# Routing in three parts of two, two and one tiles, the last attention ahead of the third projection, and two tiles' rows summed by GpSimd from a copy made by ScalarE

## The chip, the cores and the metric

One core of one Trainium2 chip runs the whole program in one launch. The metric is device time in microseconds. Of three runs of the kernel before, the median is 133.79 us (133.21 to 134.04). The engines are called as in the profile: PE (TensorE), DVE (VectorE), ACT (ScalarE), POOL (GpSimd) and SP (SyncE, which here only issues DMAs).

## The reference

A vision transformer with one layer and a routed feed-forward part, all in f32:

```python
h = patchify(x) @ W_proj.T + b_proj + pos_emb           # 16 images, 36 patches of 768 -> 256
h = concatenate([cls_tok, h])                           # 37 tokens an image, 592 in all
h = h + attention(layernorm(h))                         # 16 heads of 16, causal, 37 x 37, W_out, b_out
xn = layernorm(h)
logits = (xn @ w_red) @ normalized(wg).T                # 8 experts
idx = argmax(softmax(logits)); score = that softmax's largest value
y = gelu(xn @ w1[idx] + b1[idx]) @ w2[idx] + b2[idx]    # 256 -> 1024 -> 256
h = h + y * score
```

## The kernel before

The 592 tokens are five tiles of 128 rows, tile 0 to 4 (the last has 80 rows). The 16 images are eight **pairs**, 0 to 7 (LAST is 7). The program goes through these stages: the patch embedding; the first norm, keys, queries and values; attention pair by pair; the output projection of each tile; the routing of each tile; and the eight experts. Every engine has its own list of instructions, written out by hand, and takes them in that order. Engines meet at semaphores: `wait_ge(q["name"], n)` holds the engine's list until that semaphore has been raised n times.

**Values.** ACT copies each tile's value rows, with eight more columns `xg` (the input's share of the routing logits), to `hz[:, j, 0:264]` (`save_values`, L407). SP stores them to memory and loads them back in another layout (L335, L341), in two halves of four pairs. POOL multiplies each pair's values with a mask into `vbd` (L1118, eight instructions, the last four from the second half).

**Attention** is a loop over i from 1 to 7 on all engines. In step i PE does: scores of pair i (L609, L617), `turned` of pair i-3 (two transposes of the result, L679), `transposed` of pair i-1 (six transposes of the probabilities, L654), `attend` of pair i-2 (24 matmuls in the profile, L672), and in steps 4 and 6 `project` of tile 0 or 1 (L685). DVE takes the maximum and subtracts it (L907, L911), and divides the result of pair i-2 (`weighted`, L969, L972). ACT copies the turned result of pair i-3 out of PSUM (`save_output`, L457, two instructions), the transposed probabilities of pair i-1 (`save_probs`, L465, two) and takes the exponential of pair i (L433). The results of pairs 0 to 5 all use one PSUM bank, so `attend(u)` first waits until `ot_ready` says that ACT's `save_output` of pair u-1 is done (L664).

**Projection and routing.** For tiles 0 to 2 DVE adds the residual rows to the projection (L929); for tiles 3 and 4 PE adds them with a matmul by the identity (`own_row`, L692) and ACT copies them (`second_rows`, L412, L414). The routing logits are eight more columns of the projection; DVE adds `hG` to them (L920), which it made before with one small instruction per tile from `xg` (L994). Then `choose` finds each row's expert (five instructions), PE counts the rows ahead of each (`count_before`, L697 to L703), `keys` and `places` (L953 to L959) make the row's address and a 0/1 matrix, and `dispatch` (L715) multiplies the normalised rows by that matrix, which gives the inputs of experts 0 and 1 on the chip. This is done in two parts, tiles 0 to 2 and tiles 3 and 4. POOL takes the inverse root of each tile's variance (L1124) and writes the normalised rows (L1129). All rows also go to memory by five indirect DMAs (L1138), and SP loads them back for experts 2 to 7 (L354).

**Experts.** `hidden` (L793) and `down` (L807) on PE, with the weights of four experts held at a time. SP issues the weights of expert 4 after the row loads (L326, L327).

Of the kernel before, what the change touches and what calls it, by code (L numbers as in the profile page):

```python
# [20 lines left out]
P = 128  # L21
# [31 lines left out]
EARLY = 3  # L53
# [70 lines left out]
def vit_tower(nc, embed_in, places_in, b_proj, w_qkv, b_qk, b_v, w_out, w_out_t, b_out, b_out_c, wg, w_red_t, w1, b1, w2, b2,  # L124
              cf_d, cb_d, iota_d, out):
    ctx = ExitStack()
    with ctx:
# [142 lines left out]
        PROJ_BANK = (BZ, BZ, BZ, 1, 2)  # L270
# [6 lines left out]
        def o_bank(u):  # L277
# [9 lines left out]
            hb_ready proj_ps veps2_ready rstd2_ready shift2_ready h2_ready z_pool z_act  # L287
            loaded_woutt loaded_boutc gc_ready wg_ps hg_ready
# [101 lines left out]
        def _(act):  # L390
# [25 lines left out]

            def second_keys(a):
# [68 lines left out]
            for j in range(EARLY):  # L486
                weigh(j)
            for j in range(BY_PE, NT):
                second_rows(j)
# [3 lines left out]
            act.wait_ge(q["hot_ready"], 2)  # L493
            for j in range(EARLY, NT):
                weigh(j)
# [25 lines left out]
        def _(pe):  # L521
# [167 lines left out]
            def own_row(j):  # L689
                pe.wait_ge(q["hb_ready"], j + 1)  # L690
                pe.wait_ge(q["hg_ready"], j + 1)
                nc.tensor.matmul(ps[:, PROJ_BANK[j], 0:DV], ident, h[:, j, :], start=True, stop=False)  # L692

            def count_before(j0, j1):
# [3 lines left out]
                pe.wait_ge(q["hot_ready"], 1 if j0 == 0 else 2)  # L698
# [7 lines left out]
            def dispatch(j):  # L706
# [5 lines left out]
                pe.wait_ge(q["place32_dve"], j + 1)  # L712
                for t in range(ONCHIP):
                    for k in range(KD):
                        m = nc.tensor.matmul(ps[:, BX[t][k], 0:P], hz[:, j, D + k * P:D + (k + 1) * P],  # L715
                                             place32[:, j, t * P:(t + 1) * P], start=(j == 0), stop=(j == NT - 1))
                        if j == NT - 1:
                            m.then_inc(q["soon_ps"], 1)

            for i in range(1, PAIRS):  # L720
# [12 lines left out]
                if i in PROJ_AT:  # L733
# [4 lines left out]
                    else:  # L738
                        pe.wait_ge(q["h2_ready"], j)
# [17 lines left out]
            count_before(0, EARLY)  # L757
            pe.wait_ge(q["ot_ready"], KD * PAIRS)
            project(4)
            pe.wait_ge(q["h2_ready"], BY_PE)  # L760
            for j in range(EARLY - 1):
                dispatch(j)
            count_before(EARLY, NT)
            dispatch(EARLY - 1)
# [3 lines left out]
            for j in range(EARLY, NT):  # L768
                dispatch(j)
# [62 lines left out]
        def _(dve):  # L832
# [82 lines left out]
            def own_logits(j):  # L915
                dve.wait_ge(q["proj_ps"], j + 1)
                src = ps[:, PROJ_BANK[j], D:DV]
                if j < BY_PE:
                    dve.wait_ge(q["hg_ready"], j + 1)
# [3 lines left out]

            def second_norm(j):
                dve.wait_ge(q["proj_ps"], j + 1)
                src = ps[:, PROJ_BANK[j], 0:D]
                if j < BY_PE:
                    dve.wait_ge(q["hb_ready"], j + 1)
                    V.tensor_tensor(hz[:, j, 0:D], src, h[:, j, 0:D], ALU.add).then_inc(q["h2_ready"], 1)  # L929
                    dve.wait_ge(q["h2_ready"], j + 1)  # L930
                    src = hz[:, j, 0:D]
                norm_stats(src, stats2, mv2, veps2, j, q["veps2_ready"])

            def choose(j0, j1):
# [4 lines left out]
                dve.wait_ge(q["lg_ready"], j1)  # L939
# [9 lines left out]
            def keys(part, j0, j1):  # L949

                dve.wait_ge(q["hot_ready"], part + 1)
# [5 lines left out]
            def places(j0, j1):  # L957
                for j in range(j0, j1):
                    V.tensor_scalar(place32[:, j, :], iota[:, :], key[:, j:j + 1], None, ALU.is_equal)\  # L959
                        .then_inc(q["place32_dve"], 1)  # L960
# [23 lines left out]
            for i in range(1, PAIRS):  # L984
                softmax_top(i)
                if i == 1:
                    first_queries(1)
                if i >= 2:
                    weighted(i - 2)
                if i == 2:  # L990
                    V.tensor_tensor(std[:, :], veps[:, :], rstd[:, :], ALU.mult)
                    dve.wait_ge(q["vrow_ready"], NT)
# [8 lines left out]
            second_norm(1)  # L1001
            own_logits(2)
            choose(0, EARLY)
            weighted(LAST)
            second_norm(2)
            dve.wait_ge(q["loaded_iota"], 16)
            keys(0, 0, EARLY)
            places(0, EARLY)
            own_logits(3)
            second_norm(3)  # L1010
            own_logits(4)
            choose(EARLY, NT)
            second_norm(4)
            keys(1, EARLY, NT)
            places(EARLY, NT)
# [7 lines left out]
            scores_of(EARLY, NT)  # L1023
# [65 lines left out]
        def _(pool):  # L1089
# [32 lines left out]
            for j in range(NT):  # L1122
# [95 lines left out]
```

## Time and profile before

| | us |
|---|---|
| median of three runs | 133.79 |
| the profiled execution | 133.21 |
| its span, first to last instruction | 131.3 |
| PE busy | 123.1 (94%) |
| DVE, ACT, POOL busy | 58.2, 48.2, 41.1 |

The profile's page gives the busy time of each engine. Beside it stand views of the trace: the chain of work that ended last, and the instructions of one engine in order of time. In these a line such as `47.89 0.54 ACT L457 ... x2` is two instructions that follow each other, the first of which starts at 47.89 us, and which together take 0.54 us. Brackets give the time that the engine sat idle before, and what released it. The profiled execution is the fastest of the three runs, 0.58 us under their median.

### The profile page before, as it was taken

The numbers are of one execution on the slowest core, as the hardware profiler recorded it, in microseconds if no ns is written. First come the engines' busy times: TensorE is split into PE (matmuls) and PEld (weight loads), VectorE is DVE, ScalarE is ACT, GpSimd is POOL, SyncE is SP. The second block draws the span as 40 slices with busy tenths as digits, with TensorE's granted clock in tenths as the row PEclk, the third lists the DMA queues.
The fourth block names the chain that finished last, engine by engine and source line by source line (L and its number), as shares of the span: only waits on it lengthen the run. The fifth ranks groups of instructions, "written<-read, shape, count | busy, mean of one in ns | idle before, by whom it ended". The sixth has DMA issues, their size and how long they took to land.

```text
span 131.3 us, 2718 instructions
## 1 busy us (share of the span) xinstructions
PE 123.1 (94%) x1034; PEld 105.2 (80%) x1034; DVE 58.2 (44%) x179; ACT 48.2 (37%) x143; POOL 41.1 (31%) x52
## 2 busy tenths in 40 slices
PE   5999999999999999999899999999999999999960
PEld 1768897887667777777799998999998989999840
DVE  1231899363986898888957000522102121220210
ACT  0300002383866745662349360066042331506000
POOL 8800034850092193314847500050020202011022
PEclk9999999999999999999999999999999999999999
DMA  4899999159469999999996548999999994000000
GB/s 125 276 394 407 379 411 403 56 176 182 96 138 185 242 362 387 364 386 358 400 352 248 228 124 229 355 405 371 397 362 386 350 377 143 24 0 24 2 28 30
DMA packets 19934, 33.37 MB, mean 254 GB/s; under 512 B 1799, under 2 KB 13704, under 8 KB 19918
## 3 DMA queue, kind: packets, MB, share of 16 engines
q1 hardware_dynamic: 18382, 30.73, 70.8%
q0 software_dynamic: 768, 2.12, 4.3%
q10 hardware_dynamic: 768, 0.31, 0.9%
q8 instruction: 10, 0.16, 0.6%
q14 instruction: 6, 0.05, 0.1%
HBM read 27.75 MB, written 5.84 MB: 256 GB/s over the span
## 4 chain that ended last, share of the span: by engine, by line
PE 68%; DMA 14%; DVE 7%; issue 4%; POOL 3%; SPq 2%; ACT 1%; POOLq 0%
PE ps L793 22%; PE ps L807 19%; PE ps L524 9%; DMA w2s<-v_scratch 5%; DMA early<-embed_in 4%; DMA v_scratch<-hz 4%; PE ps L584 4%; PE ps L591 3%; POOL vbd L1118 2%; PE ps L672 2%; PE ps L685 2%; PE ps L715 2%; PE ps L654 1%; SPq L341 1%; PE ps L776 1%
## 5 line engine op out<-in xcount | busy, mean ns | idle before, releaser
L507 ACT ACTIVATE early<-ps,b1s 128x128 f32<-128x128 f32 x64 | 18.2, 370 | 31.7 <-PE ps L793 31.7
L793 PEld LDWEIGHTS ps<-early,w1s 128*128 128x128 f32 x256 | 29.4, 192 | 0.4 <-issue 0.2
L793 PE MATMUL ps<-early,w1s 128*128 128x128 f32 x256 | 29.6, 275 | 0.0
L807 PE MATMUL ps<-w2s,early 128*128 128x256 f32 x128 | 28.8, 379 | 0.0
L807 PEld LDWEIGHTS ps<-w2s,early 128*128 128x128 f32 x128 | 23.8, 190 | 2.9
L524 PE MATMUL ps<-early 128*128 128x256 f32 x60 | 15.4, 408 | 0.5 <-DMA early<-embed_in 0.5
L524 PEld LDWEIGHTS ps<-early 128*128 128x128 f32 x60 | 11.8, 204 | 3.5 <-DMA early<-embed_in 1.8
L1051 DVE COPY early<-ps 128x256 f32<-128x256 f32 x6 | 2.5, 425 | 25.9 <-PE ps L776 25.9
L1143 POOL DMA_INDIRECT out<-pos,early x4 | 3.9, 970 | 25.7 <-DVE pos L1067 25.3
L1143 POOL DMA_INDIRECT out<-pos,wide x4 | 3.9, 973 | 21.1 <-DVE pos L1067 21.1
L591 PE MATMUL ps<-xnt,wqkv 128*128 128x296 f32 x32 | 9.1, 422 | 0.0
L907 DVE TENSOR_REDUCE negmax<-ps 101x16 f32<-101x592 f32 x8 | 6.2, 772 | 4.6 <-PE ps L617 4.6
L1067 DVE SCALAR_TENSOR_TENSOR pos<-ps,wide,hsum 128x256 f32<-128x256 f32 x4 | 1.9, 483 | 14.1 <-issue 14.1
L401 ACT ACTIVATE xnt<-ps 128x256 f32<-128x256 f32 x5 | 1.7, 380 | 17.0 <-PE ps L571 17.0
L1100 POOL TENSOR_TENSOR rstd<-veps,cf 128x1 f32<-128x1 f32 x5 | 3.2, 632 | 14.4 <-DVE veps L855 14.4
L672 PEld LDWEIGHTS ps<-vbd,probst 111*64 111x64 f32 (+1 forms) x192 | 6.1, 125 | 1.6 <-issue 1.3
L457 ACT ACTIVATE ot<-ps,bv 128x74 f32<-128x74 f32 x16 | 4.3, 323 | 7.8 <-PE ps L679 7.8
L591 PEld LDWEIGHTS ps<-xnt,wqkv 128*128 128x128 f32 x32 | 5.8, 190 | 1.8 <-issue 0.2
L433 ACT ACTIVATE probs<-probs 101x592 f32<-101x592 f32 x8 | 5.6, 697 | 4.3 <-DVE probs L911 4.2
L672 PE MATMUL ps<-vbd,probst 111*64 111x51 f32 (+2 forms) x192 | 6.7, 215 | 0.4
L1118 POOL TENSOR_TENSOR vbd<-w1s,cf 111x512 f32<-111x512 f32 x4 | 4.1, 1066 | 8.0 <-DMA w1s<-v_scratch 8.0
L654 PE MATMUL ps<-cf,probs 101*111 101x101 f32 x48 | 6.1, 264 | 0.2 <-ACT probs L433 0.2
(132 smaller groups left out, 168.1 us busy)
## 6 DMA issues: line engine op xcount, KB each, us to landing
w1s<-w SPq DMA_DIRECT2D x8, 1024.0 KB, 10.7
w2s<-w SPq DMA_DIRECT2D x8, 1024.0 KB, 12.2
slot_scratch<-nil SPq DMA_DIRECT2D x1, 2560.0 KB, 15.1
early<-embed_in SPq DMA_DIRECT2D x5, 448.0 KB, 7.2
early<-slot_scratch SPq DMA_DIRECT2D x4, 320.0 KB, 5.4
wide<-slot_scratch SPq DMA_DIRECT2D x4, 320.0 KB, 6.6
b2s<-b SPq DMA_DIRECT2D x4, 256.0 KB, 8.0
wqkv<-w_qkv SPq DMA_DIRECT2D x1, 768.0 KB, 10.7
```

What stands on the lines that cost most here:

```text
L433: nc.scalar.activation(probs[:, u % 2, 0:ALLS], probs[:, u % 2, 0:ALLS], ACT.Exp).then_inc(q["probs_ready"], 1)
L507: nc.scalar.activation(gt[:, t % 2, f, :], ps[:, 2 * (t % 2) + f // 4, (f % 4) * P:(f % 4 + 1) * P], ACT.Gelu, bias=b1t[:, f:f + 1]).then_ ...
L524: return nc.tensor.matmul(ps[:, j, 0:D], emb[:, k, D + j * P:D + (j + 1) * P], emb[:, k, 0:D], start=(k == 0), stop=(k == KE - 1))
L584: m = nc.tensor.matmul(ps[:, VALUES_AT[j], 0:DV], xnt[:, k, j * P:(j + 1) * P], wqkv[:, k, 2 * D:3 * D + E], start=(k == 0), stop=(k == KD ...
L591: m = nc.tensor.matmul(ps[:, QK_BANK[a][n], 0:HALF], wqkv[:, k, col:col + P], xnt[:, k, a * HALF:(a + 1) * HALF], start=(k == 0), stop=(k ...
L654: m = nc.tensor.transpose(ps[0:GS, BP + half, g * ROWS:(g + 1) * ROWS], probs[:, u % 2, at:at + GS], ident[0:ROWS, 0:ROWS])
L672: m = nc.tensor.matmul(ps[a * ROW_B:a * ROW_B + w, o_bank(u), g * GH * VW:g * GH * VW + n], probst[:, u % 2, at:at + w], vbd[:, col:col + ...
L793: m = nc.tensor.matmul(ps[:, 2 * (t % 2) + f // 4, (f % 4) * P:(f % 4 + 1) * P], w1s[:, r, k, f * P:(f + 1) * P], xt[:, t % 2, k, :], star ...
L807: m = nc.tensor.matmul(ps[:, 4 + t % 2, 0:D], gt[:, t % 2, f, :], w2s[:, r, f, :], start=(f == 0), stop=(f == FT - 1))
L907: link(V.tensor_reduce(negmax[:, u % 2, :].rearrange("p (r h) -> p r h", r=2), s3, AX.X, ALU.max, negate=True))
L1118: pool.tensor_tensor(vbd[:, 2 * u * VI:2 * (u + 1) * VI].rearrange("p (h w) -> p h w", w=VW)[:, :, 0:DH], v3[g][:, b0:b0 + 2, :].rearrange ...
L1143: pool.indirect_dma_start(out, bass.IndirectOffsetOnAxis(row_of(t).bitcast(U32)[:, 2 * D:2 * D + 1], 0), yout[:, t % 2, :], None, bounds_c ...
```

## The change

The routing is cut in three parts: tiles 0 and 1, tiles 2 and 3, and tile 4. For tiles 0 and 1, ACT copies the projection with its eight logit columns from PSUM to `hz` right after the exponential of steps 4 and 6 (`save_projection`). POOL adds `hG` and the residual rows to that copy, which DVE did before. `hG` of all five tiles is made by POOL in two instructions, after the eight masks of the values. The copy goes where `xg` lies, so it waits until `hG` is made (`hg_ready`). The choice of tiles 0 and 1 stands in step 7 of the loop, `attend(LAST)` and `own_row(3)` stand ahead of `project(2)`, and the tiles are dispatched in the order 1, 0, 3, 2, 4.

```diff
-EARLY = 3
+PARTS = ((0, 2), (2, 4), (4, 5))
+BY_POOL = 2
+ORDER = (1, 0, 3, 2, 4)
...
 # ACT
+            def save_projection(j):
+                act.wait_ge(q["hg_ready"], 1)
+                act.wait_ge(q["proj_ps"], j + 1)
+                nc.scalar.activation(hz[:, j, 0:DV], ps[:, PROJ_BANK[j], 0:DV], ACT.Copy).then_inc(q["proj_saved"], 1)
...
                 exponentials(i)
                 if i == 2:
                     second_queries(1)
+                if i in PROJ_AT:
+                    save_projection(PROJ_AT[i])
+            save_probs(LAST)
             save_output(PAIRS - 3)
-            save_probs(LAST)
-            for u in range(PAIRS - 2, PAIRS):
-                save_output(u)
+            save_output(PAIRS - 2)
...
 # PE
             attend(PAIRS - 2)
+            transposed(LAST)
+            own_row(3)
+            count_before(0)
             turned(PAIRS - 3)
-            transposed(LAST)
+            attend(LAST)
             turned(PAIRS - 2)
-            pe.wait_ge(q["h2_ready"], 2)
-            pe.wait_ge(q["lg_ready"], 2)
+            pe.wait_ge(q["proj_saved"], BY_POOL)
             pe.wait_ge(q["ot_ready"], KD * (PAIRS - 2))
             project(2)
-            attend(LAST)
             pe.wait_ge(q["ot_ready"], KD * (PAIRS - 1))
-            own_row(3)
             project(3)
             turned(LAST)
             own_row(4)
-            count_before(0, EARLY)
             pe.wait_ge(q["ot_ready"], KD * PAIRS)
             project(4)
...
+            dispatch(1)
+            count_before(1)
+            dispatch(0)
+            dispatch(3)
+            count_before(2)
+            dispatch(2)
...
-            for j in range(EARLY, NT):
-                dispatch(j)
+            dispatch(4)
...
 # DVE
+                if i == LAST:
+                    choose(0, 2)
                 if i >= 2:
                     weighted(i - 2)
...
-                if 3 <= i:
-                    V.scalar_tensor_tensor(hG[:, i - 3, :], xg[:, i - 3, :], std[:, i - 3:i - 2], bo[:, :], ALU.mult, ALU.add)\
-                        .then_inc(q["hg_ready"], 1)
-                if i == 5:
-                    own_logits(0)
+                if i == 6:
                     second_norm(0)
             weighted(PAIRS - 2)
-            own_logits(1)
+            dve.wait_ge(q["loaded_iota"], 16)
+            keys(0)
+            places(1)
             second_norm(1)
+            weighted(LAST)
...
+            lowered(4)
             dve.wait_ge(q["count_ps"], 1)
             V.tensor_copy(cnt[:, :], cntp).then_inc(q["count_ready"], 1)
-            scores_of(0, EARLY)
+            scores_of(0, BY_PE)
...
 # POOL, after the eight masks of the values
+            pool.tensor_tensor(rtmp[:, :, :], xg[:, :, :], std[:, :].unsqueeze(2).to_broadcast([P, NT, E]), ALU.mult)\
+                .then_inc(q["xg_ready"], 1)
+            pool.wait_ge(q["xg_ready"], 1)
+            pool.tensor_tensor(hG, rtmp[:, :, :], bo[:, :].unsqueeze(1).to_broadcast([P, NT, E]), ALU.add)\
+                .then_inc(q["hg_ready"], 1)
...
+            for j in range(BY_POOL):
+                pool.wait_ge(q["proj_saved"], j + 1)
+                pool.tensor_tensor(lg[:, j, :], hz[:, j, D:DV], hG[:, j, :], ALU.add).then_inc(q["lg_pool"], 1)
+                pool.tensor_tensor(hz[:, j, 0:D], hz[:, j, 0:D], h[:, j, 0:D], ALU.add).then_inc(q["h2_pool"], 1)
```

The order on ACT around step 4 of the loop, before. `probs` is the exponential of pair 4, then comes step 5: `ot` of pair 2 and `probst` of pair 4.

```order
L433 ACTIVATE probs<-probs 101x592 [waits shifted_ready]
L457 ACTIVATE ot<-ps,bv 128x74 [waits ot_ps]
L457 ACTIVATE ot<-ps,bv 128x74
L465 ACTIVATE probst<-ps 111x303 [waits probst_ps,o_ps]
L465 ACTIVATE probst<-ps 111x303 [waits probst_ps]
```

The same place of the change:

```order
L440 ACTIVATE probs<-probs 101x592 [waits shifted_ready]
L422 ACTIVATE hz<-ps 128x264 [waits proj_ps,hg_ready]
L464 ACTIVATE ot<-ps,bv 128x74 [waits ot_ps]
L464 ACTIVATE ot<-ps,bv 128x74
L472 ACTIVATE probst<-ps 111x303 [waits probst_ps,o_ps]
L472 ACTIVATE probst<-ps 111x303 [waits probst_ps]
```

The copy L422 with its wait on `hg_ready` now stands between the exponential of pair 4 and the copies of step 5.

The order on POOL from the second half's masks on, in the change (before, L1124 follows the masks at once):

```order
L1155 TENSOR_TENSOR vbd<-w2s,cf 111x32x16 [waits loaded_v1] x4
L1162 TENSOR_TENSOR rtmp<-hz,std 128x40 [waits std_ready,wg_ready,vrow_ready]
L1165 TENSOR_TENSOR h<-rtmp,bo 128x5x8 [waits xg_ready]
L1171 TENSOR_TENSOR lg<-hz,h 128x8 [waits proj_saved,hb_ready,hg_ready]
L1172 TENSOR_TENSOR hz<-hz,h 128x256
L1171 TENSOR_TENSOR lg<-hz,h 128x8 [waits proj_saved]
L1172 TENSOR_TENSOR hz<-hz,h 128x256
```

L1165 raises `hg_ready`; it stands behind all four masks of the second half.

The end of PE's list ahead of the experts, in the change. L665 is `transposed(7)`, L703 `own_row`, L709 to L715 `count_before`, L690 `turned`, L696 `project`, L727 `dispatch`, L781 the count of all rows, L807 the first expert.

```order
L690 MATMUL ps<-cf,o 128x101 x2
L703 MATMUL ps<-h,cf 128x264
L696 MATMUL ps<-wout,ot 128x264 x2
L727 MATMUL ps<-wide,hz 128x128 x4
L709 MATMUL ps<-cb 128x16
L713 MATMUL ps<-hotb,cb 128x16 x2
L713 MATMUL ps<-hotb,cb 128x8
L715 MATMUL ps<-hotb,cb 128x16
L727 MATMUL ps<-wide,hz 128x128 x8
L709 MATMUL ps<-cb 128x8
L713 MATMUL ps<-hotb,cb 128x8 x4
L715 MATMUL ps<-hotb,cb 128x8
```

Between the second count and the third now stand eight matmuls of `dispatch`; before, the second count followed eight of them and only four stood behind it.

## Rows read from the trace of the kernel before

**Rows 1.** The page's busy times: us, share of the span, instructions.

```profile
PE 123.1 (94%) x1034; PEld 105.2 (80%) x1034; DVE 58.2 (44%) x179; ACT 48.2 (37%) x143; POOL 41.1 (31%) x52
```

**Rows 2.** The chain that ended last, its expert stage: start, us, what.

```profile
69.08 7.38 PE ps L793 x64
...
94.63 3.57 PE ps L793 x32
...
119.94 4.44 PE ps L807 x21
```

**Rows 3.** PE's weight loads in order of time, with the idle time before them.

```profile
48.50 0.77 PEld L672 LDWEIGHTS ps<-vbd,probst 111*64 111x64 f32 x24 [0.23 <-POOL vbd L1118]
...
56.62 0.20 PEld L679 LDWEIGHTS ps<-cf,o 101*128 101x128 f32 x2 [0.23 <-DVE o L972]
...
57.78 0.74 PEld L685 LDWEIGHTS ps<-wout,ot 128*128 128x128 f32 x4 [0.20 <-DVE hz L929]
...
62.08 0.74 PEld L685 LDWEIGHTS ps<-wout,ot 128*128 128x128 f32 x4 [0.17 <-ACT ot L457]
...
65.45 0.17 PEld L701 LDWEIGHTS ps<-hotb,cb 128*128 128x128 bf16 x4 [0.51 <-DVE hotb L946]
...
66.95 1.90 PEld L715 LDWEIGHTS ps<-wide,hz 128*128 128x128 f32 x16 [0.21 <-issue]
```

**Rows 4.** POOL's instructions in order of time, masks and routing.

```profile
24.63 3.47 POOL L1112 TENSOR_TENSOR h<-h,bout 128x256 f32<-128x256 f32 x5
...
45.35 4.12 POOL L1118 TENSOR_TENSOR vbd<-w2s,cf 111x512 f32<-111x512 f32 x4 [5.11 <-DMA w2s<-v_scratch]
...
65.12 0.26 POOL L1132 TENSOR_SCALAR shift<-mv,rstd 128x1 f32<-128x1 f32 x1
66.23 0.65 POOL L1124 TENSOR_TENSOR rstd<-veps,cf 128x1 f32<-128x1 f32 x1 [0.85 <-DVE veps L855]
...
68.38 1.22 POOL L1138 DMA_INDIRECT slot_scratch<-hz,keyu  x1 [1.13 <-issue]
```

**Rows 5.** ACT's instructions in order of time, step 4 to step 5.

```profile
45.40 0.70 ACT L433 ACTIVATE probs<-probs 101x592 f32<-101x592 f32 x1
47.89 0.54 ACT L457 ACTIVATE ot<-ps,bv 128x74 f32<-128x74 f32 x2 [1.80 <-PE ps L679]
48.32 0.74 ACT L465 ACTIVATE probst<-ps 111x303 f32<-111x303 f32 x2
49.23 0.70 ACT L433 ACTIVATE probs<-probs 101x592 f32<-101x592 f32 x1 [0.16 <-DVE probs L911]
```

**Rows 6.** PE's matmuls in order of time.

```profile
3.57 3.52 PE L524 MATMUL ps<-early 128*128 128x256 f32 x10 [0.24 <-DMA early<-embed_in]
7.38 2.43 PE L524 MATMUL ps<-early 128*128 128x256 f32 x10 [0.29 <-DMA early<-embed_in]
...
48.53 0.84 PE L672 MATMUL ps<-vbd,probst 111*64 111x51 f32 x24
...
65.57 0.17 PE L703 MATMUL ps<-hotb,cb 128*128 128x16 bf16 x1
```

**Rows 7.** DVE's instructions in order of time.

```profile
46.38 1.07 DVE L994 SCALAR_TENSOR_TENSOR h<-hz,std,bo 128x8 f32<-128x8 f32 x1
...
50.06 0.22 DVE L994 SCALAR_TENSOR_TENSOR h<-hz,std,bo 128x8 f32<-128x8 f32 x1
...
59.18 0.18 DVE L940 TENSOR_REDUCE lmax<-lg 128x3 f32<-128x24 f32 x1
...
60.20 0.18 DVE L946 TENSOR_TENSOR hotb<-cf,best 128x24 bf16<-128x24 f32 x1
...
67.17 0.17 DVE L964 RECIPROCAL hz<-esum 128x3 f32<-128x3 f32 x1
```

**Rows 8.** SP's DMA issues, and the landing of expert 4's second weights (issue at 82.77).

```profile
82.77 0.47 SPq L327 DMA_DIRECT2D w2s<-w  x1
...
DMA to landing us min/median/max: 10.9/10.9/10.9
```

More of the change, by code:

```diff
@@ L480, in _ @@
                     second_queries(1)
+                if i in PROJ_AT:
+                    save_projection(PROJ_AT[i])
+            save_probs(LAST)
             save_output(PAIRS - 3)
-            save_probs(LAST)
-            for u in range(PAIRS - 2, PAIRS):
-                save_output(u)
+            save_output(PAIRS - 2)
             act.wait_ge(q["hot_ready"], 1)
[L486 to L489, printed above, removed]
+            weigh(0)
+            save_output(LAST)
+            weigh(1)
+            second_rows(3)
+            act.wait_ge(q["hot_ready"], 2)
+            weigh(2)
+            second_rows(4)
+            weigh(3)
             for t in range(ONCHIP):
@@ L715, in dispatch @@
                         m = nc.tensor.matmul(ps[:, BX[t][k], 0:P], hz[:, j, D + k * P:D + (k + 1) * P],
[L716 to L717 removed]
+                                             place32[:, j, t * P:(t + 1) * P],
+                                             start=(j == ORDER[0]), stop=(j == ORDER[-1]))
+                        if j == ORDER[-1]:
                             m.then_inc(q["soon_ps"], 1)
@@ L756, in _ @@
             own_row(4)
-            count_before(0, EARLY)
             pe.wait_ge(q["ot_ready"], KD * PAIRS)
             project(4)
-            pe.wait_ge(q["h2_ready"], BY_PE)
-            for j in range(EARLY - 1):
-                dispatch(j)
-            count_before(EARLY, NT)
-            dispatch(EARLY - 1)
+            pe.wait_ge(q["h2_ready"], 1)
+            pe.wait_ge(q["lg_ready"], 1)
+            dispatch(1)
[4 more added lines that the diff above has]
+            dispatch(2)
             for j in range(NT):
@@ L767, in _ @@
             m.then_inc(q["count_ps"], 1)
-            for j in range(EARLY, NT):
-                dispatch(j)
+            dispatch(4)
             def turn_rows(t):
@@ L918, in own_logits @@
                 if j < BY_PE:
-                    dve.wait_ge(q["hg_ready"], j + 1)
+                    dve.wait_ge(q["hg_ready"], 1)
                     V.tensor_tensor(lg[:, j, :], src, hG[:, j, :], ALU.add).then_inc(q["lg_ready"], 1)
@@ L947, in choose, with choose_last, lowered, keys @@
                     .then_inc(q["hot_ready"], 1)
-            def keys(part, j0, j1):
+            def choose_last(j):
+                dve.wait_ge(q["lg_ready"], j - BY_POOL + 1)
+                src = lg[:, j, :]
+                link(V.tensor_reduce(lmax[:, j:j + 1], src, AX.X, ALU.max))
+                link(V.scalar_tensor_tensor(prio[:, j, :], src, lmax[:, j:j + 1], C("revval")[:, j * E:(j + 1) * E],
+                                            ALU.is_equal, ALU.mult))
+                link(V.tensor_reduce(best[:, j:j + 1], prio[:, j, :], AX.X, ALU.max))
+                V.tensor_scalar(hotb[:, j, :], C("revidx"), best[:, j:j + 1], None, ALU.is_equal).then_inc(q["hot_ready"], 1)
+            def lowered(j):
+                V.tensor_scalar(low[:, j, :], lg[:, j, :], lmax[:, j:j + 1], None, ALU.subtract)\
+                    .then_inc(q["low_ready"], 1)
+            def keys(part):
+                j0, j1 = PARTS[part]
                 dve.wait_ge(q["hot_ready"], part + 1)
@@ L955, in keys, with places @@
                 link(V.tensor_reduce(key[:, j0:j1], rtmp[:, j0:j1, :], AX.X, ALU.add))
[L957 to L960, printed above, removed]
+            def places(j):
+                V.tensor_scalar(place32[:, j, :], iota[:, :], key[:, j:j + 1], None, ALU.is_equal)\
+                    .then_inc(q["place32_dve"], 1)
             def scores_of(j0, j1):
@@ L1121, in _, with inverse @@
                     C("vmask")[0:GS, :].unsqueeze(2).to_broadcast([GS, 2 * HEADS, DH]), ALU.mult).then_inc(q["v_ready"], 1)
-            for j in range(NT):
+            pool.wait_ge(q["vrow_ready"], NT)
+            pool.wait_ge(q["wg_ready"], 1)
+            pool.wait_ge(q["std_ready"], 1)
+            pool.tensor_tensor(rtmp[:, :, :], xg[:, :, :], std[:, :].unsqueeze(2).to_broadcast([P, NT, E]), ALU.mult)\
[3 more added lines that the diff above has]
+                .then_inc(q["hg_ready"], 1)
+            pool.wait_ge(q["hg_ready"], 1)
+            pool.wait_ge(q["hb_ready"], NT)
+            for j in range(BY_POOL):
+                pool.wait_ge(q["proj_saved"], j + 1)
+                pool.tensor_tensor(lg[:, j, :], hz[:, j, D:DV], hG[:, j, :], ALU.add).then_inc(q["lg_pool"], 1)
+                pool.tensor_tensor(hz[:, j, 0:D], hz[:, j, 0:D], h[:, j, 0:D], ALU.add).then_inc(q["h2_pool"], 1)
+            def inverse(j):
                 pool.wait_ge(q["veps2_ready"], j + 1)
```

94 lines of the change are left out of this document (57 added, 37 removed).

## The prediction

> **What bounds the kernel now.** I read the page's busy times first. PE is busy 94% of the span, DVE 44%, ACT 37%, POOL 31% [rows 1]: a change can gain only what PE waits, and it loses whatever makes PE wait. Second, the chain of waits. From 69.08 us on, where the first expert begins, to 124.37 it is PE alone, row behind row [rows 2]. So the time is the start of the first expert plus a fixed rest, as long as the weights arrive in time. The question is what the change does to the 69.08. Third, PE's weight loads between 48 and 69 us with the idle time before them, since a weight load is the first thing to start after a wait. The waits ahead of the experts which this change touches are 0.23 us for DVE's result of pair 5, 0.20 for DVE's row sum, 0.17 for ACT's last copy, 0.51 for the second choice of experts and 0.21 before the last dispatch [rows 3], 1.32 us in all. That is the most that the new order can give back. Last, ACT and POOL in order of time around 45 to 50 us [rows 4, 5], because the change puts a new wait of ACT on POOL there.
>
> **The new wait on ACT.** `save_projection(0)` is issued on ACT behind the exponential of step 4, which ends at 45.40 + 0.70 = 46.10 us [rows 5]. It waits for `hg_ready`. That is raised by the second of two POOL instructions which stand behind the last four masks. These masks can't start before their data is loaded: POOL sat idle 5.11 us for it, started at 45.35 and ended at 49.47 [rows 4]. None of this changes, so the two instructions start at about 49.5.
>
> Their size is 128 x 40, which POOL doesn't show. The nearest rows below and above are 0.26 us for 128 x 1 and 3.47 / 5 = 0.69 for 128 x 256 [rows 4]. Drawn straight between them, 40 elements are 0.33 us; I take that, as 40 lies far nearer the small one. The ends of the bound are 0.26 and 0.69. So `hg_ready` comes at 49.47 + 0.05 + 0.33 + 0.04 + 0.33 = 50.22 us, with bounds 50.1 and 50.9. [...]
>
> What is queued behind that wait on ACT: the two copies of pair 2's result, which ran from 47.89 to 48.43, then the two copies of pair 4's probabilities and the exponential of pair 5 [rows 5]. PE's `attend(3)` waits for the first of these, since its PSUM bank must be empty; it started at 48.53, 0.10 us after the copies ended, with 0.23 us of idle before its first weight load [rows 3, 6]. (That row names POOL as the releaser; the wait is for several semaphores, and the one raised last before it is ACT's copy.) In the change: the new copy starts at 50.25; the next one can follow 0.30 us later (two copies of 303 columns take 0.74, so one holds the next back for about 0.74 / 2 less the overlap [rows 5]); the two copies of pair 2 take 0.54; `attend(3)` starts at 50.25 + 0.30 + 0.54 + 0.10 = 51.19. **The stall is 51.19 - 48.53 = 2.66 us**, of which nothing is hidden: PE has no other work issued ahead of it in its list. With the bounds of POOL's two instructions it is 2.5 to 3.4.
>
> Does the loop catch up? Behind `attend(3)` the same PE instructions follow in the same order up to `attend(6)`. ACT's exponential of pair 5 would end at about 51.0 + 0.62 + 0.70 = 52.3, and PE asks for it only some 1.9 us behind the start of `attend(3)`, at 53.1; covered. DVE has slack there and gets some work less. So PE isn't late a second time, but it doesn't catch up either, since it is the bound: all of the 2.66 us arrive at the end of the loop. The second copy (step 6) costs nothing: `hG` is done, and ACT has idle time there.
>
> The Trainium skill (PSUM — Partial Sum Buffer, section Engine vs sequencer instructions) says that the queues of ScalarE, VectorE and GpSimdE are strictly first in, first out. The rows of ACT stand in the order of its list, so the trace agrees as far as it can. If an engine could let the pair's copies pass, the stall would be nil.
>
> **What DVE loses and POOL gains.** One small instruction of DVE on two tensors took 1.07 us while POOL wrote masks, and the same 0.22 later [rows 7]. These instructions leave DVE: no gain in time, because DVE waits in both places. POOL's four new sums for tiles 0 and 1 (up to 0.69 us each, two of them small) fall where POOL sat idle.
>
> **The end of the loop and the routing.** Of the 1.32 us of waits:
> - The 0.23 at 56.62 is traded: `transposed(7)` now comes right behind `attend(6)`, without the `turned` between them that covered the last exponential, and waits about as long. Nothing gained.
> - The 0.20 at 57.78 goes: the copy of tile 1 is done long before. What is late next is ACT's copy of pair 5, which PE reaches later than before.
> - The 0.17 at 62.08 stays: ACT's copy of the last pair still stands between the last `turned` and `project(4)`.
> - The 0.51 at 65.45 goes: the choice for tiles 2 and 3 doesn't wait for tile 4 any more, and `dispatch(1)` and the work before it cover it.
> - The 0.21 at 66.95 goes: eight matmuls of dispatch cover the addresses of tile 3, and four and the count those of tile 4.
>
> That is 0.92. Against it stand four more counting matmuls (14 for 10; a run of them shows 0.17 us for four weight loads [rows 3], so 0.15 together) and one more break of PE's stream at each of two places, 0.1 each, taken from the 0.10 between copy and `attend`. Net gain 0.6 us; the bounds are 0 (a break for every wait that goes) and 1.3 (all the waits). The choice in step 7 takes DVE 60.20 + 0.18 - 59.18 = 1.2 us [rows 7] ahead of `weighted(5)`; own_row(3) and the last transposes cover it on PE. If they don't, `turned(5)` waits up to 0.5, which is inside the bound.
>
> **The weights.** Expert 4's second weights landed 82.77 + 10.9 = 93.67 us [rows 8], and its first matmul was at 94.63 [rows 2]: 0.96 us to spare. Their issue hangs on POOL's first row DMA, at 68.38, that is 1.04 us behind the reciprocal of the scores at 67.34 [rows 4, 7], and 0.70 ahead of the first expert. In the change only one dispatch (about 0.9 us) stands behind the last address, where two stood, and the counts must be in before the scores. So the row DMAs come some 0.75 us later against the experts. The spare time falls to about 0.2: no cost, but up to 0.3 us in the upper bound.
>
> **The sum.** +2.66 - 0.6 = +2.06 us. On the profiled execution, 133.21 us, that makes 135.3; against the median of the runs, 133.79, it makes **135.8 us**, and that I forecast. Its own range: 2.5 - 1.3 = +1.2 gives 135.0; 3.4 - 0 + 0.3 = +3.7 gives 137.5.
>
> **Rivals.**
> 1. *The stall comes, and the routing gives back all its waits*: +2.5 - 1.3 = +1.2, about 135.0 us. For it: three of the five waits already lose their cause. Against: the 0.17 has no cover, and the new wait for the exponential has none either. Chance 0.15.
> 2. *ACT doesn't wait; not slower.* The one mechanism: the second half of the values lands early. The stall is the landing plus 4.12 us of masks plus 0.7, so it shrinks by one us for each us that the landing is before 45.28 or so. From a landing at 42.6 on there is none, and the gain of the routing is left: 133.79 - 0.6 = 133.2 us (132.5 if all waits go). Against: the DMA is issued behind the same work as before, and nothing that the change touches comes earlier. Chance 0.07.
> 3. *PE's clock falls in the pause.* PE would sit idle for 2.7 us. The longest idle of PE in rows 3 is 0.51 us, so no row speaks of such a pause. For the price, the nearest rows are two groups of ten equal matmuls near the start, 3.52 us and 2.43 us [rows 6]; the first group may owe a part of that to the lower level (1.2 GHz) and a part to its data. Over one such stretch it is +1.1 us, twice that if it lasts, so 136.9 to 138.0 us. The Trainium skill (TensorE: Matmul & The Clock Gate, section Why this matters for your kernels) warns that idle gaps between bursts cost the clock. Chance 0.06.
>
> **Chances.** My case 0.72, the rivals 0.15, 0.07 and 0.06. What a measurement can tell from no change is 1%, here below 132.45 or above 135.13. Faster by over 1%: 0.03, from rival 2's far end. Within 1%: rival 1 for the most part, the rest of rival 2 and the lowest edge of my case, 0.22. Slower by over 1%: 0.75. The range leaves out rival 2, half of rival 3 and the tails of my case: 134.5 to 137.3 us.
>
> **What the changed profile would show.** ACT idle for some 4 us before the copy of L422, released by POOL's L1165 at about 50.2; POOL's two instructions directly behind the masks; PE idle for 2.5 to 3 us before the attend of pair 3, at about 51.2; the first expert at about 71.1 instead of 69.08; no long wait before the second counting; the expert stage as long as before, 55.3 us from its start to its last matmul. I am wrong if `hG` is ready before 48 us, if PE's idle time before the experts comes back in other places, if POOL's two small instructions take a microsecond each, or if PE waits for the weights of expert 4.

## The result: 139.27 us, slower, and outside the range

| | before | after |
|---|---|---|
| median of six runs each, us | 133.55 (133.00 to 134.43) | 139.27 (137.81 to 141.22) |
| ratio | | 1.0338 [1.0295, 1.0381] |
| the profiled execution, us | 133.21 | 138.59 |
| its span, us | 131.3 | 136.7 |

The change makes the kernel slower, as forecast, but by more than twice as much: 135.8 us was predicted, 2.0 above the kernel before, with a range of 134.5 to 137.3, and it is 4.5 us by the ratio or 5.7 by the medians. The ratio is lower than that of the medians (1.043), because it leaves out three runs of the changed kernel that lie more than 1.5% above its fastest, though their mean granted clocks (0.955 to 0.966) are like that of one that it keeps (0.957).

The case for which I gave 0.72 (ACT stalls, and that is all) is not what happened. The stall came, and then the third rival, PE's clock, for which I gave 0.06 and whose price I put too low.

### The stall

ACT's instructions of the changed kernel in order of time (start, us, engine, line, what, and in brackets the idle time before and its releaser):

```profile
45.15 0.70 ACT L440 ACTIVATE probs<-probs 101x592 f32<-101x592 f32 x1
49.68 0.39 ACT L422 ACTIVATE hz<-ps 128x264 f32<-128x264 f32 x1 [3.84 <-POOL h L1165]
49.97 0.53 ACT L464 ACTIVATE ot<-ps,bv 128x74 f32<-128x74 f32 x2
```

POOL's, same kernel:

```profile
44.98 4.11 POOL L1155 TENSOR_TENSOR vbd<-w2s,cf 111x512 f32<-111x512 f32 x4 [4.88 <-DMA w2s<-v_scratch]
49.05 0.26 POOL L1162 TENSOR_TENSOR rtmp<-hz,std 128x40 f32<-128x40 f32 x1
49.38 0.27 POOL L1165 TENSOR_TENSOR h<-rtmp,bo 128x40 f32<-128x40 f32 x1
```

This is the picture of [rows 4, 5] with the new wait in it. The four masks end at 49.09, the two small instructions make `hG` by 49.65, and the copy L422, idle for 3.84 us before, starts at 49.68. The two copies of pair 2's result, which ran at 47.89 before [rows 5], now run at 49.97. They are `attend(3)`'s release. PE's matmuls, same kernel:

```profile
44.59 0.84 PE L683 MATMUL ps<-vbd,probst 111*64 111x51 f32 x24
...
50.60 1.43 PE L683 MATMUL ps<-vbd,probst 111*64 111x51 f32 x24 [2.42 <-issue]
51.97 0.46 PE L620 MATMUL ps<-cb 64*64 64x296 bf16 x4
...
54.98 1.46 PE L683 MATMUL ps<-vbd,probst 111*64 111x51 f32 x24
56.38 2.13 PE L696 MATMUL ps<-wout,ot 128*128 128x264 f32 x4
...
61.00 1.54 PE L683 MATMUL ps<-vbd,probst 111*64 111x51 f32 x48
```

And before, of which the row at 48.53 stands in [rows 6]:

```profile
44.85 0.84 PE L672 MATMUL ps<-vbd,probst 111*64 111x51 f32 x24
...
51.27 0.84 PE L672 MATMUL ps<-vbd,probst 111*64 111x51 f32 x24
52.04 1.16 PE L685 MATMUL ps<-wout,ot 128*128 128x264 f32 x4
...
54.95 1.54 PE L672 MATMUL ps<-vbd,probst 111*64 111x51 f32 x48
```

The rows are `attend` of pair 2 (44.85), of pairs 3 and 4, and of pairs 5 and 6 in one row (54.95). Read two things here. First, the place of the idle time: 2.42 us stand in the brackets ahead of `attend(3)`, where the matmuls of the kernel before have no bracket at all. Second, the same 24 matmuls take 1.43 and 1.46 us instead of 0.84, and `project(1)` takes 2.13 instead of 1.16. No wait explains that: the instructions themselves have become longer.

### The clock

The changed kernel in stretches (columns: stretch in us, its length, busy time and instructions of PE, PEld, DVE, ACT, POOL, granted clock, DMA share, GB/s):

```profile
45.00:50.00 5.00, 3.18 (x48) 2.37 (x43) 2.34 (x5) 1.13 (x4) 4.57 (x6) 0.99 1.06 371
50.00:55.00 5.00, 4.40 (x54) 3.82 (x54) 2.16 (x4) 2.66 (x9) 0.89 (x2) 0.50 1.06 374
55.00:60.00 5.00, 5.00 (x50) 3.68 (x50) 1.46 (x7) 1.42 (x4) 0.93 (x3) 0.50 1.06 378
60.00:65.00 5.00, 4.91 (x95) 4.44 (x95) 4.42 (x15) 3.13 (x9) 1.71 (x2) 0.99 1.06 388
```

And the kernel before:

```profile
50.00:55.00 5.00, 4.75 (x71) 3.70 (x68) 4.57 (x14) 2.55 (x8) 1.79 (x2) 1.00 1.05 373
55.00:60.00 5.00, 4.86 (x88) 4.11 (x89) 4.07 (x16) 2.77 (x9) 1.21 (x2) 1.00 1.05 377
```

From 50 to 60 us the granted clock of the changed kernel is 0.50, the lower of the two levels (1.2 GHz), where the kernel before has 1.00. The clock fell in the pause ahead of `attend(3)` and came back ten microseconds later, while PE was 94% busy (4.40 + 5.00 of 10).

### The account of the profiled executions

| stretch of PE | before | after | difference |
|---|---|---|---|
| start to `attend(2)` | 44.85 | 44.59 | -0.26 |
| `attend(2)` to `attend(3)`: the pause | 3.68 | 6.01 | +2.33 |
| `attend(3)` to `attend(5)`: at the lower clock | 6.42 | 10.40 | +3.98 |
| `attend(5)` to the first expert: the routing | 14.13 | 13.39 | -0.74 |
| the first expert to the end of the span | 62.2 | 62.3 | +0.1 |
| the span | 131.3 | 136.7 | +5.4 |

The first expert starts at 74.39, where 69.08 stood [rows 2] and 71.1 was forecast.

### The profile page after: what moved, and what is told of

Same layout as the page of the kernel before. It is cut to its first block, busy times and chain, and to the rows that moved or that the text cites. A ratio compares the mean times of both kernels' runs of the same rounds, so it can differ in the third digit from the quotient of the medians.

```text
span 136.7 us, 2734 instructions
## 1 busy us (share of the span) xinstructions
PE 127.0 (93%) x1038; PEld 108.5 (79%) x1038; DVE 56.8 (42%) x177; ACT 49.0 (36%) x145; POOL 42.9 (31%) x58
## 4 chain that ended last, share of the span: by engine, by line
PE 70%; DMA 11%; issue 8%; POOL 7%; SPq 2%; ACT 1%; POOLq 0%; DVE 0%
PE ps L807 21%; PE ps L821 18%; PE ps L535 8%; POOL vbd L1155 6%; DMA w1s<-v_scratch 5%; DMA early<-embed_in 4%; PE ps L683 4%; PE ps L727 4%; PE ps L696 4%; PE ps L595 2%; DMA v_scratch<-hz 2%; PE ps L665 2%; PE ps L628 1%; PE ps L690 1%; SPq L343 1%
## 5 line engine op out<-in xcount | busy, mean ns | idle before, releaser
L807 PEld LDWEIGHTS ps<-early,w1s 128*128 128x128 f32 x256 | 29.4, 192 | 0.4 <-issue 0.2
L807 PE MATMUL ps<-early,w1s 128*128 128x128 f32 x256 | 29.6, 275 | 0.0
L683 PE MATMUL ps<-vbd,probst 111*64 111x51 f32 (+3 forms) x192 | 7.9, 234 | 2.7 <-issue 2.4
L683 PEld LDWEIGHTS ps<-vbd,probst 111*64 111x64 f32 (+1 forms) x192 | 7.3, 143 | 3.6 <-issue 3.4
L665 PE MATMUL ps<-cf,probs 101*111 101x101 f32 x48 | 6.8, 282 | 0.2 <-ACT probs L440 0.2
L472 ACT ACTIVATE probst<-ps 111x303 f32<-111x303 f32 x16 | 6.0, 428 | 1.6 <-PE ps L665 1.5
```

Source lines behind the costliest of these rows:

```text
L472: nc.scalar.activation(probst[:, u % 2, half * GH * ROWS:(half + 1) * GH * ROWS], ps[0:GS, BP + half, 0:GH * ROWS], ACT.Copy).then_inc(q[" ...
L665: m = nc.tensor.transpose(ps[0:GS, BP + half, g * ROWS:(g + 1) * ROWS], probs[:, u % 2, at:at + GS], ident[0:ROWS, 0:ROWS])
L683: m = nc.tensor.matmul(ps[a * ROW_B:a * ROW_B + w, o_bank(u), g * GH * VW:g * GH * VW + n], probst[:, u % 2, at:at + w], vbd[:, col:col + ...
L807: m = nc.tensor.matmul(ps[:, 2 * (t % 2) + f // 4, (f % 4) * P:(f % 4 + 1) * P], w1s[:, r, k, f * P:(f + 1) * P], xt[:, t % 2, k, :], star ...
```

## The experiments

Theory A: the loss is the pause, by its own length, and then the lower clock that it brings about. Theory B: the late `hG` costs all of it by what waits behind it, whatever the clock does. Theory C: the new order of the routing, or the work moved to POOL, is dear in itself. (The expectations below, which were written before each run, use the letter B for more than one rival; each says which it means.) The runs of the kernel before beside these have medians of 133.61 to 134.04 us. One of them, beside the last two kernels, took 432.36 us; it moves their median by less than 0.1.

### `hG` ahead of the second half's masks

The two instructions of POOL become a function, and are called behind the fourth mask, not the eighth.

```diff
+                if u == 3:
+                    own_share()
```

> The changed kernel, with POOL's two instructions for hG put behind the fourth mask of the values instead of the eighth, so that hg_ready comes at about 41 us and ACT finds it raised. Theory A (the wait of ACT on hG makes PE pause 2.3 us, the pause costs the clock, together 6.3 us; the new routing gives 0.7 us back): 139.3 - 6.3 = about 133.0 us, some 0.7 us under the kernel before, granted clock 1.0 throughout. Theory B (the slow stretch from 50 to 60 us has another cause in the change, POOL's and ACT's new work beside PE): only the 2.3 us go, about 137 us, and the clock still falls.

Measured: 133.60 us (133.12 to 135.01, ten runs), ratio 1.0018 [0.9974, 1.0061]. The whole loss goes. The copy and `attend(3)` in the profile of this kernel:

```profile
47.19 0.39 ACT L422 ACTIVATE hz<-ps 128x264 f32<-128x264 f32 x1 [0.77 <-PE ps L696]
```

```profile
48.81 0.77 PEld L683 LDWEIGHTS ps<-vbd,probst 111*64 111x64 f32 x24 [0.23 <-issue]
...
81.76 0.20 PEld L790 LDWEIGHTS ps<-cf,early 128*128 128x128 f32 x2 [0.95 <-DMA early<-slot_scratch]
...
94.83 2.31 PEld L807 LDWEIGHTS ps<-early,w1s 128*128 128x128 f32 x20 [0.26 <-DMA w2s<-w]
```

The clock is 1.00 from 50 to 60 us. So the rival that POOL's and ACT's new work beside PE slows it falls: that work is all still there. Now the copy waits for PE's own projection, and `attend(3)` for the usual 0.23 us. From `attend(5)`, at 55.26, to the first expert, at 68.65, it is 13.39 us, to the hundredth what the changed kernel shows, so the routing's gain of 0.74 is real. It doesn't reach the end: PE's weight loads wait 0.95 us for the rows that come back from memory (L790) and 0.26 for expert 4's second weights, and from the first expert to expert 4's first matmul it is 26.18 us (68.65 to 94.83), where it was 25.39 (69.08 to 94.47). That speaks against C as far as the order of the routing goes, but shows that the order costs something behind it.

### The copy into another buffer

The same, undone in the other place: `hG` stays behind the eighth mask, and ACT copies to a free part of `early`, so that it needs no `hG`.

```diff
-                act.wait_ge(q["hg_ready"], 1)
-                nc.scalar.activation(hz[:, j, 0:DV], ps[:, PROJ_BANK[j], 0:DV], ACT.Copy).then_inc(q["proj_saved"], 1)
+                nc.scalar.activation(pj[:, j, :], ps[:, PROJ_BANK[j], 0:DV], ACT.Copy).then_inc(q["proj_saved"], 1)
```

> The changed kernel, with ACT's copy of the projection written to memory that nothing else uses then, so that it has no need to wait for hG; hG stays late on POOL, behind the eighth mask. Theory A: what counts is ACT's wait, not when POOL makes hG: as with the early hG, about 133.0 us and full clock. Rival C (late hG holds something else up too, such as own_row(3) or the choice of experts): 0.5 us or more above the kernel with the early hG, with PE idle before own_row(3) or the first count.

Measured: 133.76 us (133.07 to 134.92, ten runs), ratio 1.000 [0.9967, 1.0033]. `hG` is as late as in the change, and nothing is lost: only ACT's wait for it costs. The first expert is at 68.39 us, and the waits for rows and weights are 1.03 and 0.59.

### `hG` on POOL, and nothing else

The kernel before, with `hG` made by POOL behind the fourth mask.

```diff
-                if 3 <= i:
-                    V.scalar_tensor_tensor(hG[:, i - 3, :], xg[:, i - 3, :], std[:, i - 3:i - 2], bo[:, :], ALU.mult, ALU.add)\
-                        .then_inc(q["hg_ready"], 1)
...
+                if u == 3:
+                    own_share()
```

> The kernel before, with hG of all tiles made by POOL in two instructions behind the fourth mask and nothing else, so that DVE loses its five small ones. Both theories: no change, 133.6 us, since DVE waits where these stood; first expert at 69.1 us from the span's start as before. If DVE's work in the loop did count, up to 0.5 us less.

Measured: 133.73 us (132.95 to 134.25, ten runs), ratio 1.0025 [1.0000, 1.0051]. Moving these instructions from DVE to POOL is worth nothing; by the interval it costs between nothing and 0.5%.

### The pause kept, the clock held

The changed kernel, with ten idle matmuls of PE ahead of `attend(3)`. (Each is two rows of the profile, hence x20.)

```diff
+                if i == 5:
+                    pe.wait_ge(q["shifted_ready"], 5)
+                    for _ in range(10):
+                        nc.tensor.matmul(ps[:, 0, 0:P], ident, ident, start=True, stop=True)
```

> The changed kernel, with ten idle matmuls of 128 x 128 (2.2 us at full clock) on PE where it pauses, into a PSUM bank that is free then; the wait of ACT stays. Theory A, with the clock as a cost of its own: the clock stays at 1.0 and the 4.0 us of slow PE go, the 2.3 us of waiting stay: 139.3 - 4.0 = about 135.2 us, some 1.7 us above the kernel before. Theory B (the clock has nothing to do with the pause): about 139.3 us as the changed kernel.

Measured: 136.26 us (135.64 to 136.91, four runs), ratio 1.0210 [1.0159, 1.0261]. PE's matmuls in the profile of this kernel:

```profile
48.33 2.42 PE L744 MATMUL ps<-cf 128*128 128x128 f32 x20
51.47 0.84 PE L683 MATMUL ps<-vbd,probst 111*64 111x51 f32 x24 [0.72 <-issue]
...
54.21 0.84 PE L683 MATMUL ps<-vbd,probst 111*64 111x51 f32 x24
```

```profile
50.00:55.00 5.00, 4.12 (x84) 3.49 (x82) 2.23 (x4) 3.42 (x11) 1.33 (x4) 1.00 1.05 377
```

`attend(3)` is as late as ever (51.47), but it takes 0.84 us, and the clock is 1.00. Adding work to PE made the changed kernel faster: 3.0 us by the medians, 1.2% by the two ratios. `attend(3)` to `attend(5)` is 6.42 us again, the first expert at 71.28, which is within 0.2 us of what the prediction's own account gave (71.1). What is left against the kernel before is the pause with its routing gain, plus 0.43 us of waiting for expert 4's weights.

### The pause alone, and the same with the clock held

The kernel before, with a pause of the same kind and none of the rest: `hG` on POOL behind the eighth mask, and in step 4

```diff
+                if i == 4:
+                    act.wait_ge(q["hg_ready"], 1)
+                    nc.scalar.activation(pj[:, :], bout[:, :], ACT.Copy)
```

> The kernel before with the wait alone: POOL makes hG in two instructions behind the eighth mask, and ACT waits for it behind the exponential of step 4 and then makes one copy of 256 columns that nobody needs; routing and order as before. Theory A: + 2.3 us of pause + 4.0 us of slow clock: 133.55 + 6.3 = about 139.9 us, 0.7 us above the changed kernel. Theory B: + 2.3 us, about 135.9 us.

Measured: 140.06 us (136.76 to 140.65, four runs; no ratio is on record). The profile of this kernel, PE and then stretches:

```profile
51.53 1.44 PE L676 MATMUL ps<-vbd,probst 111*64 111x51 f32 x24 [2.99 <-issue]
...
55.91 1.46 PE L676 MATMUL ps<-vbd,probst 111*64 111x51 f32 x24
```

```profile
50.00:55.00 5.00, 3.47 (x48) 3.07 (x49) 1.84 (x8) 2.15 (x7) 0.47 (x2) 0.55 1.05 375
55.00:60.00 5.00, 5.00 (x46) 3.90 (x48) 2.14 (x5) 1.98 (x5) 1.78 (x2) 0.50 1.06 379
```

So the old order of the routing doesn't protect: with the pause alone the loss is 6 us and more in three of the four runs, as large as that of the whole change. This time by itself doesn't tell A from B, so the same kernel was run with the ten idle matmuls:

> The kernel before with attention(3)'s pause alone (hG on GpSimd behind the eighth mask, ScalarE waits for it in step 4 and makes an idle copy), and ten idle 128x128 matmuls of TensorE put into the pause. The idle matmuls and the copy compute nothing that is used. Theory A (the pause costs its own length, some 2.3 to 2.8 us, and the rest of the loss is the half clock that follows the pause): the matmuls break the pause, the granted clock stays at its full level, and the time is 133.6 + 2.5 = 136.1 (135.6 to 136.8). Theory B (the late hG costs some 6 us by what waits behind it, whatever the clock does): 139 to 140.5 as in the same kernel without the matmuls.

Measured: 136.18 us (135.40 to 138.04, five runs), ratio 1.0178 [1.0129, 1.0226], and a mean clock of 0.992 to 1.000 in all of them. A had said 136.1 and B 139 to 140.5. In the profile the stretch from 50 to 55 us has a clock of 1.00 and `attend(3)` comes at 53.50 (its values landed later in this execution, the longest of the five). B falls: the wait costs 2.1 us by the medians and 2.4 by the ratio, and all above that is the clock.

### How long a pause it takes

Two runs with `hG` made earlier in the second half, behind its second mask (the sixth) and its third (the seventh):

```diff
+                if u == 5:
+                    own_share()
```

> The same behind the sixth mask: the pause is about 0.3 us longer than without the wait, and the clock stays up. About 133.9 us or, where the later first expert only takes up the wait for the rows from memory (0.95 us in the run with hG behind the fourth mask), 133.6 us.

> The changed kernel, with the two instructions for hG behind the seventh mask: ACT's wait, and PE's pause, are 1.0 us shorter than in the change (one mask), so some 1.3 us. Theory A, if a pause of that length costs the clock: 133.6 (hG after the fourth mask) + 1.3 + up to 4.0 = 138.9 us. If it doesn't: 133.6 + 1.3 = about 134.9 us, less what the late rows give back, clock 1.0.

Measured: 134.08 us (133.36 to 135.04, ten runs), ratio 1.0050 [1.0020, 1.0080], for the sixth; 136.32 us (134.87 to 139.82, five runs), ratio 1.0220 [1.0182, 1.0258], for the seventh. The matmuls of `attend(3)`, the sixth first:

```profile
49.04 0.84 PE L683 MATMUL ps<-vbd,probst 111*64 111x51 f32 x24 [0.63 <-issue]
```

```profile
50.76 0.84 PE L683 MATMUL ps<-vbd,probst 111*64 111x51 f32 x24 [1.91 <-issue]
```

And the changed kernel with five idle matmuls in place of ten:

> The changed kernel with five idle 128x128 matmuls in place of ten ahead of attention(3)'s own; they compute nothing that is used. A pause of some 1.3 us should be left behind them. If the clock falls only after the whole pause of 2.5 us and more, the time is that of the ten matmuls, 136.3 (135.6 to 136.9), at a mean clock of 0.99. If a pause of 1.3 us suffices, about 4 us more, 139 to 140.5, at a mean clock of 0.96. Something between, with some runs on either side, would say that the boundary lies near such a pause.

Measured: 136.02 us (135.82 to 136.70, five runs), ratio 1.0155 [1.0109, 1.0201]. The pause was not the 1.3 us that I expected:

```profile
48.51 1.30 PE L744 MATMUL ps<-cf 128*128 128x128 f32 x10
51.98 0.84 PE L683 MATMUL ps<-vbd,probst 111*64 111x51 f32 x24 [2.17 <-issue]
```

The second half of the values had landed later in this execution (the masks started at 46.35, not 44.98). Yet the clock stayed at 1.00 in the stretches that follow. The mean clock of every single run tells the rest (the runs of the kernel before have 0.990 to 1.000):

| kernel | pause in its profile, us | runs, us (mean clock) |
|---|---|---|
| sixth mask | 0.63 | 133.36 to 135.04 (0.991 to 1.000), ten |
| ten idle matmuls | 0.72 | 135.64 to 136.91 (0.992 to 0.997), four |
| before, pause, ten idle | 1.14 | 135.40 to 138.04 (0.992 to 1.000), five |
| seventh mask | 1.91 | 134.87 (0.997), 135.99 (0.992), 136.32 (0.992), 136.50 (0.984), 139.82 (0.959) |
| five idle matmuls | 2.17 | 135.82 to 136.70 (0.995 to 1.000), five |
| the change | 2.42 | 137.81 (0.986), 138.13 (0.982), 138.59 (0.957), 139.95 (0.955), 139.98 (0.966), 141.22 (0.963) |
| before, pause alone | 2.99 | 136.76 (0.981), 139.92 (0.955), 140.20 (0.956), 140.65 (0.956) |

The pause is known for the profiled run of each kernel only. In the kernels with up to 1.14 us no run lost the clock. In those with 2.4 us and above every run did, three of ten for a shorter stretch, to go by their mean (0.98), and seven for the long one (0.96). In between it is a matter of the run. What decides there (a pause that differs from run to run, or where in time it falls) these runs don't separate.

### A version that beats both

In the first experiment's kernel the rows came back late. Here the rows of tiles 0 and 1 go to memory before the addresses of tiles 2 and 3 are made: their addresses are cast and their scores inverted apart.

```diff
+            V.tensor_copy(keyu[:, 0:BY_POOL], key[:, 0:BY_POOL]).then_inc(q["keyu_ready"], 1)
+            scores_of(0, BY_POOL)
...
-                pool.wait_ge(q["score_ready"], 1 if j < BY_PE else 2)
+                pool.wait_ge(q["keyu_ready"], 1 if j < BY_POOL else 2)
+                pool.wait_ge(q["score_ready"], 1 if j < BY_POOL else 2 if j < NT - 1 else 3)
```

> hG behind the fourth mask, and the rows of tiles 0 and 1 go to memory as soon as their addresses and scores are known, by one more cast and one more reciprocal on DVE ahead of the last tile's keys. Theory D (the 0.74 us that the new routing gains ahead of the experts are lost again because the rows and then expert 4's weights arrive later against the experts, 0.95 + 0.26 us of waits in the profile with hG behind the fourth mask): both waits go, about 132.5 us, 1.2 us under that kernel and 1.2 under the kernel before. Rival E (those waits only overlap with something that ends later anyway): 133.6 us, no change.

Measured: 132.87 us (132.31 to 133.30, twelve runs), ratio 0.9941 [0.9916, 0.9966]: 0.6% faster than the kernel before, by an interval that leaves out 1. POOL's first row DMA and the two weight loads that waited:

```profile
67.57 1.22 POOL L1212 DMA_INDIRECT slot_scratch<-hz,keyu  x1 [1.47 <-issue]
```

```profile
81.08 0.36 PEld L790 LDWEIGHTS ps<-cf,early 128*128 128x128 f32 x2
...
94.06 3.09 PEld L807 LDWEIGHTS ps<-early,w1s 128*128 128x128 f32 x26
```

The first row DMA is at 67.57, where it was at 68.92 in the first experiment, SP issues the row loads at 75.77 instead of 78.56, and no bracket stands behind either weight load.

## Why the prediction was wrong, by its own steps

**What bounds the kernel.** Right for the change: the start of the first expert plus a fixed rest, 62.2 and 62.3 us. The rest isn't fixed once rows and weights come late: 63.3 us in the first experiment (131.9 - 68.65).

**The new wait on ACT.** Right in mechanism and place. POOL's two instructions took 0.26 and 0.27 us against 0.33 predicted; from the end of the masks to `hG` it was 0.56 us, not 0.75. From the end of the masks to `attend(3)` it was 49.09 to 50.60, 1.51 us against 1.72. The stall was 2.33 us against 2.66. (The sum's 0.05, 0.04 and 0.10 us between instructions are small and the first two stand in no row.) ACT idled for 3.84 us with the copies of pair 2 ready behind the wait (their transposes ended at 47.6), so it doesn't let them pass; that agrees with the Trainium skill's rule of strict order (PSUM — Partial Sum Buffer, section Engine vs sequencer instructions).

**"Nothing is hidden, and PE doesn't catch up."** Right about catching up. But this step took every instruction behind the pause at its old length. It is here that the prediction failed. The 6.42 us of work between `attend(3)` and `attend(5)` took 10.40, because the granted clock was 0.50.

**Rival 3, the clock.** This is the same failed step as a rival, wrong in its chance and in its price. The chance was 0.06 because no row of the kernel before has such a pause. That was absence of evidence, and I read it as evidence against. By my judgement now, an unbounded unknown that the change itself creates should have had a third of the chance or more. The price, +1.1 us or twice that, was taken from one stretch of ten matmuls [rows 6]; the fall lasted for 10 us of the loop and cost 3.98. The same two rows come nearer if the slowdown is applied to all that PE does while the clock is low: 3.52 / 2.43 = 1.45, and measured it was 10.40 / 6.42 = 1.62, so 2.9 us against 3.98. Even that would have been luck in part: the profile of the kernel before has a granted clock of 1.00 from 3.5 to 7.1 us, so no row shows that the first group owed its length to the clock. What I lacked was how long it lasts, and an upper end had to be put there. The rule of the Trainium skill (TensorE: Matmul & The Clock Gate, section Why this matters for your kernels), that idle gaps between bursts cost the clock, agrees with the trace in kind: 2.42 us of idle, then 0.50 for two stretches of 5 us. The idle time here was shorter than the gaps of which the page warns, and the measurement decides.

**The routing.** -0.6 predicted, -0.74 measured, and not by the list of waits as I had it. PE's weight loads of the changed kernel:

```profile
62.47 0.66 PEld L665 LDWEIGHTS ps<-cf,probs 101*111 101x111 f32 x6
...
67.79 0.74 PEld L696 LDWEIGHTS ps<-wout,ot 128*128 128x128 f32 x4 [0.57 <-ACT ot L464]
...
70.94 0.97 PEld L727 LDWEIGHTS ps<-wide,hz 128*128 128x128 f32 x8 [0.19 <-issue]
```

Against [rows 3]: `transposed(7)` has no wait at all, where I had it trade 0.23; the 0.17 ahead of the last projection, which I let stay, became 0.57; the 0.51 ahead of the second count went as forecast; the 0.21 of the dispatch is 0.19, in another place. Three waits of the same view I didn't count at all: 0.34 ahead of `attend(7)` at 58.87, 0.21 at 61.06 and 0.23 at 63.06. They are gone in the change, so 1.32 us was not the most that the order could give. Over the whole stretch the brackets of the weight loads fall from 2.10 us to 0.76, and only 0.74 of that arrives. So the size was right in part by luck, because errors of both signs cancel.

**The weights.** Right for the profiled execution of the change, and wrong for the kernel with the early `hG`. In the change, expert 4's second weights landed at 88.08 + 11.5 = 99.6 us, some 0.3 ahead of its first matmul at 99.85, where I had 0.2; the rows of expert 2, which come from memory through the same DMAs and which I didn't price, were 0.25 us late for a weight load at 86.81, and PE lost hardly anything by it: 25.46 us from the first expert to expert 4, against 25.39 before. In the first experiment the same weights landed at 82.76 + 12.0 = 94.8 us, 26.1 behind the first expert where it was 24.6, so 1.5 us later and not 0.75; the spare time was gone, with 0.26 us of waiting, and the rows were 0.95 us late before that. POOL's first row DMA was behind the first expert in both kernels (68.92 against 68.65, 74.67 against 74.39); before, it was 0.70 ahead [rows 2, 4]. So this shift is 1.0 us in both, and how late the data land behind it is what differs. By the medians the routing's gain of 0.74 us was worth nothing in the first experiment (ratio 1.0018), and had I been right about the clock I would have been wrong here. The last kernel fits this as the whole reason: with the rows sent earlier, both waits are gone and its ratio is worth 0.79 us of 133.61.

**The sum.** -0.26 + 2.33 + 3.98 - 0.74 + 0.1 = +5.4 us in span, against +2.06. Without the clock's term it would be +1.4, less than the forecast, since the stall was over-priced by 0.33 and the routing gave 0.14 more. The changed kernel with the clock held, by five or ten idle matmuls, took 1.55% and 2.10% more than before, 2.1 and 2.8 us of 133.55: the values landed later in their profiles (masks from 46.35 and 45.85 us, not 44.98). Both times, 136.02 and 136.26, are inside the range.

## What to carry to other kernels

When a change makes PE wait in the middle of a busy stretch, price the pause twice: by its length, and by a stretch at the lower clock behind it, which here was the dearer of the two (3.98 us for a pause of 2.42). If the pause can't be removed, idle matmuls in it can be worth their place: ten of them took the loss from 5.7 to about 2.7 us (medians 139.27 and 136.26, against 133.55). A copy whose target is held by another engine's late work is best moved to another buffer, or that work put ahead of what it doesn't need: each of the two removed the whole loss. And a gain ahead of a stage of fixed length counts only as far as the transfers that this stage waits for come earlier too.

## What the runs showed of the hardware that was not expected

- The granted clock fell to 0.50 after a single pause of 2.42 us in a kernel whose PE is busy for 93% of the span, and stayed there until 60 us although PE was busy for 9.40 of the next 10 us.
- The lower clock costs some 4 us of these 10, less than the half that a doubling of every duration would cost: `attend` takes 1.7 times as long (1.43 for 0.84), `project` 1.8 times (2.13 for 1.16), and the stretch as a whole 1.62 times.
- The time from the last row DMA on POOL to SP's first row load varied: 73.75 to 76.58 us before, 74.29 to 78.56 in the first experiment, 80.05 to 83.74 in the change, 72.94 to 75.77 in the last kernel, so 2.83, 4.27, 3.69 and 2.83 us. Over all twelve kernels it is 2.83 to 3.21 us where POOL's first row DMA starts ahead of the first expert, and 3.11 to 4.27 where it starts behind. Why was not tried.
- The same masks of the second half started at 44.98 us in one kernel's profile and at 47.86 in another's, by when their data landed. A wait that hangs on such a landing has a length that differs from run to run; that the clock behind it differs for this reason is likely, and not shown.
